# Attention-and-experts block: depthwise convolution moved to TensorE, windows paired, v placed by ScalarE

## What is computed

```
qkv = einsum('oi,bihw->bohw', qkv_w, xh); q, k, v = split(qkv, 3)
lepe = conv_general_dilated(v, lepe_w, (1, 1), 'SAME', feature_group_count=c)
attn = softmax(einsum('nhqc,nhkc->nhqk', q * scale, k) + bias)
out = einsum('nhqk,nhkc->nhqc', attn, v) + lepe        # windows of 16 tokens, 8 heads
x = x + out(plain) + unroll(out(rolled))
t = t + sum over the 2 best experts of gate * (norm(t) @ expert_w + expert_b)
```

## Time and profile before

| | |
|---|---|
| median of 3 runs | 3483.31 us (3472.05 to 3487.70) |
| profiled execution, span | 3495.3 us; its own time stands nowhere else |
| busy: PE, DVE, ACT, POOL | 3038.4, 3088.6, 2038.3, 2932.3 us |
| busy share of PEld | 54% |
| mean granted TensorE clock | 0.925 |
| DMA | 469.79 MB, 427432 packets |

### The profile page before, as it was taken

The page is one execution under the profiler, slowest core; times in us unless marked ns, Lnnn a source line. Parts: engine busy times, 40 slices in busy tenths (PEclk is TensorE's granted clock), DMA queues, the critical chain, the costliest instruction groups (busy, mean ns, idle before and its releaser), DMA issues.

```text
span 3495.3 us, 200950 instructions
## 1 busy us (share of the span) xinstructions
PE 3038.4 (87%) x82372; PEld 1892.0 (54%) x82372; DVE 3088.6 (88%) x6049; ACT 2038.3 (58%) x4130; POOL 2932.3 (84%) x5382
## 2 busy tenths in 40 slices
PE   5889888888898888998888988889899899889886
PEld 3655555555555555555555555555555555555551
DVE  3789999889999888998999889999899899999995
ACT  3666666556565556665666656566556656666651
POOL 5998888888898788987888878889788988888970
PEclk8999999999899899998999989999899989999986
DMA  2345555545555455545555544555455555555555
GB/s 58 85 122 147 137 143 138 143 130 143 136 144 139 125 144 137 145 130 133 136 139 140 139 131 130 143 135 143 130 140 138 143 134 145 137 143 137 138 124 151
DMA packets 427432, 469.79 MB, mean 134 GB/s; under 512 B 117616, under 2 KB 407920, under 8 KB 426480
## 3 DMA queue, kind: packets, MB, share of 16 engines
q1 hardware_dynamic: 260592, 342.97, 36.3%
q0 software_dynamic: 165888, 113.57, 13.5%
HBM read 264.97 MB, written 77.86 MB: 98 GB/s over the span
## 4 chain that ended last, share of the span: by engine, by line
PE 36%; DVE 22%; issue 14%; DMA 12%; SPq 9%; POOL 3%; ACT 3%; DVEq 1%; ACTq 0%; POOLq 0%
PE bank L585 9%; PE bank L652 8%; SPq L454 6%; DMA gate_wide<-gate_rows 6%; DVE lepe L896 6%; DMA z<-fin 5%; PE bank L570 5%; DVE row_max L904 3%; PE bank L658 2%; PE bank L612 2%; POOL vx L528 2%; PE bank L624 2%; DVE probT L969 2%; SPq L449 1%; DVE gx L884 1%
## 5 line engine op out<-in xcount | busy, mean ns | idle before, releaser
L528 POOL DMA_DIRECT2D vx<-vt x3072 | 1555.5, 515 | 201.9 <-PE bank L658 181.0
L652 PEld LDWEIGHTS bank<-probT,vx 128*32 128x32 f32 x36864 | 825.8, 188 | 442.4 <-issue 378.2
L652 PE MATMUL bank<-probT,vx 128*32 128x16 f32 x36864 | 888.2, 234 | 170.7 <-issue 117.5
L516 POOL DMA_DIRECT2D kx<-k_sb x1536 | 738.8, 488 | 230.9 <-issue 114.6
L585 PEld LDWEIGHTS bank<-kx,qx 32*32 32x32 f32 x36864 | 602.9, 112 | 434.9 <-issue 432.2
L585 PE MATMUL bank<-kx,qx 32*32 32x64 f32 x36864 | 709.9, 227 | 128.5 <-issue 90.9
L742 ACT ACTIVATE prob<-prob 128x512 f32<-128x512 f32 x576 | 367.4, 638 | 538.9 <-DVE prob L909 538.6
L896 DVE SCALAR_TENSOR_TENSOR lepe<-vpad,table,lepe 128x384 f32<-128x384 f32 x960 | 630.8, 657 | 0.0
L884 DVE TENSOR_TENSOR gx<-gate_wide,yn_pair 128x768 f32<-128x768 f32 x384 | 393.8, 1026 | 194.4 <-DMA gate_wide<-gate_rows 148.0
L547 POOL TENSOR_TENSOR lepe_p<-lepe_p,tap_sb 128x384 f32<-128x384 f32 x384 | 435.0, 1133 | 39.0 <-issue 18.5
L904 DVE TENSOR_REDUCE row_max<-bank 128x32 f32<-128x512 f32 x576 | 394.4, 685 | 29.5 <-PE bank L585 16.4
(11 more groups left out here) (75 smaller groups left out, 3801.9 us busy)
## 6 DMA issues: line engine op xcount, KB each, us to landing
gate_wide<-gate_rows SPq DMA_DIRECT2D x768, 192.0 KB
vx<-vt POOLq DMA_DIRECT2D x3072, 12.0 KB
kx<-k_sb POOLq DMA_DIRECT2D x1536, 24.0 KB
z<-fin SPq DMA_DIRECT2D x192, 192.0 KB, 4.3
yn_pair<-yn POOLq DMA_DIRECT2D x384, 96.0 KB
xa<-in_x SPq DMA_DIRECT2D x192, 96.0 KB, 3.3
xn<-xa SPq DMA_DIRECT2D x192, 96.0 KB
xs<-xn SPq DMA_DIRECT2D x96, 192.0 KB
```

Of the source, the lines that this page charges most:

```text
L516: pool.dma_start(kx[to + m:to + C:4, r % 2, m, :], k_sb[at + m:at + C:4, r % 2, :])\
L528: pool.dma_start(vx[to:to + TOK, r % 2, col:col + 13:4, odd, :], vt[at:at + TOK, r % 2, x::2, :, :].rearrange("p h n k -> p h (n k)"))\
L652: last = MM(bank_o[32 * c:32 * c + 32, at * TOK:(at + 1) * TOK], vx[:, kr % 2, :, at % 2, at // 2 * 4 + ba], probT[:, kr % 2, at, ba * TOK ...
```

## The change

The convolution becomes 12 matmuls a tile on TensorE (`conv`, 4 in each of three slots: one for each column offset, two groups of taps, two halves of the image's width). They work on the normalised x: `conv_w` holds v's weights times the taps, made once at the start, and `halo` holds 10 rows of x, twice, one row apart, so that one matmul takes two rows of taps. The plain and the rolled convolution are added in the weights. The first and last tile of an image take other weights at some rows and are cut in pieces (`conv_rows`). The result is added to y from its own bank (`bank_c`), and VectorE makes three additions of a tile (y_first, y_second, y_third) in place of two. All that carried the taps leaves: `wo`, `vpad`, the tap products, GpSimd's additions, the multiply-adds and `add_taps`.

The 8 windows of a unit are now 4 of the left half of the image and the 4 that lie half a width to the right. A block of the turned probabilities then holds two windows (squares), and the weights of a product matmul are 32 floats in a row. The zeros of `vx` are no longer left by DMAs of parts: ScalarE copies all of v into its place by 8 copies a strip with a mask (1 or 0 per partition) as the scale, 3, 3 and 2 of them in three slots, between the exponential and the placing of the bias. Product and scores are written in pieces of 4 x 4 and 4 x 16 floats. The row sums take 8 matmuls of half the columns.

Bank g goes to the convolution, so turned logits and turned gates use p1, the gates in one transpose of 48 columns, and `logits` moves from slot 42 to 44. x, the output and z have a layout in halves, so that a tile loads by 5 DMAs (7 in the first tile) and stores by 1; the halo takes 2 loads (4 at an image's edges).

```diff
 LAG = dict(
...
-    tap_products=15, pool_taps=16, taps=19, add_taps=24,
-    store_z=24, load_tile=33, y_first=37, y_second=38, tile_sum=39, tile_variance=40, router=41, logits=42,
-    take_logits=43, gates=45, gap_exp=46, turn_gates=47, pair_yn=47, store_gates=48, spread_gates=49,
+    store_z=24, load_halo=29, load_tile=33, conv=34, y_first=37, y_second=38, y_third=38, tile_sum=39, tile_variance=40, router=41, logits=44,
+    take_logits=44, gates=45, gap_exp=46, turn_gates=47, pair_yn=47, store_gates=48, spread_gates=49,
...
-        vx = sb("vx", [128, 2, 32, 2, WIN // 2 * 4])
+        vx = sb("vx", [128, 2, PAIRED, HEADS, 32])
...
-                if st := s.strip("spread_v"):
-                    k, r = st
-                    wait_alone(pool, vt_made, k + 1)
...
-                                pool.dma_start(vx[to:to + TOK, r % 2, col:col + 13:4, odd, :],
-                                               vt[at:at + TOK, r % 2, x::2, :, :].rearrange("p h n k -> p h (n k)"))\
-                                    .then_inc(v_spread[r % 2], 16)
...
                     MM(bank_p[0][:, 0:SPX], wv, xs[:, r % 4, :], start=True, stop=True).then_inc(v_made, 1)
-                    if r % 2:
-                        pe.wait_ge(ln_made, tiles_to(s, (k - 1) // 2 + 3))
-                    MM(bank_p[1][:, 0:SPX], wo, xs[:, r % 4, :], start=True, stop=True).then_inc(vo_made, 1)
...
+                if (ti := s.in_tile("conv")) and ti[2] < len(SIDES):
+                    k, r, side = ti
...
+                    for group, skip in ((0, 0), (1, 2)):
+                        for top, end, which in conv_rows(t)[group]:
+                            for y_ in range(2):
+                                low, high = y_ * HALFW + max(0, -dw - y_), (y_ + 1) * HALFW - max(0, dw + y_ - 1)
+                                last = MM(by_rows(bank_c[y_ * C:(y_ + 1) * C, 0:SPX], HALFW)
+                                          [:, top:end, low - y_ * HALFW:high - y_ * HALFW],
+                                          conv_w[:, which, group * 3 + side, :],
+                                          by_rows(halo[:, r % 2, :], W)[:, top + skip:end + skip, low + dw:high + dw],
+                                          start=first[y_], stop=(side == 2 and group == 1), skip_group_check=True)
...
-                    for w in range(UW):
-                        at = (j * UW + w)
-                        for c in range(4):
-                            ba = c % 2 * 2 + c // 2
-                            last = MM(bank_o[32 * c:32 * c + 32, at * TOK:(at + 1) * TOK],
-                                      vx[:, kr % 2, :, at % 2, at // 2 * 4 + ba],
-                                      probT[:, kr % 2, at, ba * TOK:(ba + 1) * TOK], start=True, stop=True)
+                    for n in range(j * UPAIR, (j + 1) * UPAIR):
+                        for a in range(2):
+                            cols = slice(a * (SPX // 2), (a + 1) * (SPX // 2))
+                            for m in range(4):
+                                last = MM(out_window(bank_o[32 * m:32 * m + 32, cols], n), vx[:, kr % 2, n, m * 2 + a, :],
+                                          probT[:, kr % 2, n, m, a * TOK:(a + 1) * TOK]
+                                          .rearrange("p (i x) -> p i x", x=SP), start=True, stop=True)
...
                     S.activation(prob[:, r % 4, :], prob[:, r % 4, :], ACT.Exp).then_inc(exp_made, 1)
+                if st := s.in_strip("spread_v"):
...
+                    for part in range(3 * j, min(3 * j + 3, V_PARTS)):
+                        g, y_ = part // 2, part % 2
+                        at, col = slice(g * CH, g * CH + CH), y_ * TOK + g * HD
+                        S.activation(vx[at, r % 2, :, :, col:col + HD].rearrange("p n k h -> p (n k) h"),
+                                     vt[at, r % 2, :, :, :].rearrange("p n k h -> p (n k) h"), ACT.Copy,
+                                     scale=const("mask_v")[at, y_:y_ + 1]).then_inc(v_spread, 1)
                 if u := s.unit("place_bias"):
...
-                if st := s.in_strip("tap_products"):
...
-                if taps:
-                    tap(taps[0], taps[1], 2 * taps[2] + 1)
```

More of the change, by code:

```diff
@@ L48 @@
 UNITS = WIN // UW
+PAIRED = WIN // 2
+UPAIR = UW // 2
+HALFW = W // 2
 UPX = UW * TOK
@@ L206, in lay_tables @@
         rows = slice(g * CH, (g + 1) * CH)
-        for h in range(HD):
-            for m in range(HEADS):
-                a, b, y = m // 4, m // 2 % 2, m % 2
+        for place in range(HEADS):
+            a, m = place // 4, place % 4
+            head = (place - roll * ROLL) % HEADS
+            for h in range(HD):
                 for part, name in ((0, "wq"), (1, "wk")):
-                    put(name, rows, g * CH + a * 16 + h * 4 + m % 4, qkv_w[part * CH + h * HEADS + m])
-                here = (h - 1) % HD if roll and a and b else h
-                one = qkv_w[2 * CH + here * HEADS + m]
-                put("wv", rows, g * CH + h * 8 + y * 4 + b * 2 + a, one)
-                at = (a * 2 + b) * CH + roll * 16 + h * 4 + half * 2 + y
-                put("wo", rows, at, one)
-                put("taps", at, slice(0, 9), lepe_w[here * HEADS + m].reshape(9))
@@ L226, in lay_tables @@
     order = tile_channels()
+    for col, channel in enumerate(order):
+        half, o = channel // CH, channel % CH
+        for roll, name in ((0, "plain"), (ROLL, "rolled")):
+            own = (o - roll) % CH
+            for i in range(CH):
+                for copy in range(2):
+                    put("v_" + name, copy * C + (half * CH + i + roll) % C, col, qkv_w[2 * CH + own, i])
+            taps = lepe_w[own].reshape(3, 3)
+            for side in range(3):
+                dw = SIDES[side] + 1
+                put("taps_" + name, slice(0, C), side * C + col, taps[0, dw])
+                put("taps_" + name, slice(C, 128), side * C + col, taps[1, dw])
+                put("taps_" + name, slice(0, C), (3 + side) * C + col, taps[2, dw])
```

345 lines of the change are left out of this document (187 added, 158 removed).

## The result

The changed kernel takes 3820.45 us (median of 4 runs) where the kernel before took 3485.51 in the same session: ratio 1.0948, 95% interval 1.091 to 1.0985. The changed kernel is slower, as forecast, but by 9.5% and not by the 2.1 to 2.5% forecast; 3811 lies outside the range of 3430 to 3750 us. The profiled execution has a span of 3800.9 us.

What follows compares the result with a forecast made beforehand. It took VectorE, TensorE and GpSimd as close together, none alone at its limit; afterwards TensorE's work 2976 + ends 75.5 + loop turns 48 + ScalarE waits 385 + small waits 85 = 3570 us, range 3430 to 3750.

Steps and rivals of the forecast that it cites:

- TensorE's own work: TensorE's 3038.4 us, less v product 157.4, gate transposes 34 and faster product 346, plus convolution 475: 2976 us.
- pipeline's ends: TensorE idle in the pipeline's first 80 and last 105 us: 75.5 us, kept from the profile before.
- TensorE waits for ScalarE (bias, k copy): Scores waiting for the placed bias and the tile-sum matmul for bank p1: 4.0 us a tile, 385 us.
- loop turns: TensorE idle where the loop turns to the next image: about 6.9 us each, seven turns, 48 us.
- small waits: A quarter of TensorE's other 333 us of waits stays as semaphore waits, 85 us; the rest ends with VectorE's load.
- The mechanism, its two places: ScalarE's copies between exponential and bias stall TensorE at score matmuls and the tile-sum matmul, some 3 to 5 us a tile.
- the experts' pair as the model: Two experts' matmuls of the convolution's shape take 0.80 us, so six pairs a tile take 4.8 us.
- Rival 3: Product and score matmuls that write in pieces are slower: 3935 us, chance 0.07.
- Rival 2: Weights in a row give nothing, as their loads lie behind other work: 3743 us, chance 0.11.
- the six slots: ScalarE's path against TensorE's work per slot of a tile: waits 2.0 (value), 1.2 (tile sum), 0.8 us (variance), others nothing.
- second value slot: The value slot with two convolution pairs: TensorE's 4.2 us of work against ScalarE's 4.0, so no wait.
- rival 1: Weights in a row gain more and copies cost less, so the kernel gets faster: 3400 to 3460 us, chance 0.24.

Runs made afterwards that it cites:

- copies_last: The changed kernel with the eight copies into vx moved from before the placing of the bias to the end of ScalarE's slot: 3539.81 us, ratio 1.0171.
- whole_rows: The changed kernel with product and score matmuls writing whole rows instead of pieces, results in wrong places: 3811.73 us, ratio 1.0917.
- strided: The changed kernel, copies unchanged, with TensorE reading a product's weights 96 floats apart from the same buffer, so wrong values: 3870.55 us, ratio 1.1101.
- copies_full: The changed kernel with each of the eight copies over all 128 partitions, using an eight-column mask: 3736.96 us, ratio 1.0751.
- before_in_row: The kernel before, with only TensorE's reading of a product's weights changed to 32 columns in a row, so wrong values: 3493.26 us, ratio 1.0029.
- best: last_k with the copies over all 128 partitions and the bias placed just ahead of the exponential: 3458.34 us, ratio 0.9884.
- last_k: copies_last with ScalarE's k copy put ahead of the two q copies of its slot: 3494.95 us, ratio 1.0016.
- few_conv: The changed kernel with 10 of the 12 convolution matmuls of a tile left out: 3707.09 us, ratio 1.0625.
- apart_rows: The changed kernel with vx's 32 columns stored outside, weights 96 floats apart, and copies reading in pieces and writing whole rows: 4206.36 us, ratio 1.2052.

## Why the prediction was right in direction and wrong in size

The forecast was 3570 us. Its sum against the profiled span of 3800.9 us, term by term:

| term | forecast | measured |
|---|---|---|
| TensorE's own work | 2976 | 3013.6 |
| pipeline's ends | 75.5 | 77.1 |
| TensorE waits for ScalarE (bias, k copy) | 385 | 504.9 |
| loop turns | 48 | 31 |
| small waits | 85 | 174 |

The ends come from two windows of the changed kernel (0 to 80 and 3690 to 3801 us), 191.00 - 113.88, which answer to the earlier trace rows; 8 us of the waits for ScalarE lie in these windows too. The small waits are what is left of the span.

```profile
sum 191.00, PE 113.88 PEld 53.55 DVE 79.99 ACT 52.69 POOL 29.80; mean PE 56.94 PEld 26.78 DVE 39.99 ACT 26.34 POOL 14.90
```

**Right.** The mechanism, its two places, and the side: copies_last shows it by moving nothing else. As forecast came VectorE under 2458 us (2233.6), GpSimd under 1377 (937.2), the copies near 0.6 us long (0.604), the convolution's 475 us (482.5), the experts' pair as the model for it. Rival 3 is refuted by whole_rows. The Trainium skill, "PSUM — Partial Sum Buffer", section "Specifications (TRN2)", would have these pieces slow the matmuls significantly. The trace does not agree: 742 against 739 us for the scores. Rival 2 falls with the product's 468 us. By the rule of the Trainium skill, "TensorE: Matmul & The Clock Gate", section "LDWEIGHTS (loading the stationary operand)", that a load's time goes by its columns, loads of 32 columns would last equally long. The traces do not agree: they take 157 ns in strided and 115 ns with the columns in a row.

**Wrong: the waits for ScalarE.** The step that failed most is the one on the six slots, with the copy's spacing of 0.51: 385 us forecast, 504.9 measured. In the tile shown above, value slot 2.31 us (forecast 2.0), tile sum 1.28 (1.2), variance 1.47 (0.8), second value slot 0.66 (nothing). Both sides of each comparison were off.

- ScalarE's path was longer. Value matmul to score takes 1852.85 - 1848.52 = 4.33 us and 1871.04 - 1866.67 = 4.37, not 4.0; variance matmul to score 1864.85 - 1860.34 = 4.51, not 4.2. The exponential and three copies take 2.29 us to the bias's start (1852.10 - 1849.81), not 2.07. The forecast took the copy's price from tap products that all begin at the same partition; copies_full, with the partitions alone changed, shows 69 to 74 us for that.
- TensorE had less to do meanwhile. The second value slot's 4.2 us were 3.67 (1848.52 to 1851.38 + 0.81), the variance slot's 3.4 were 3.04 (1860.34 to 1862.54 + 0.84). The main reason is the product: 468.2 / 576 = 0.81 us a unit instead of 0.94, and 0.60 from its first matmul to the next instruction (1851.38 - 1850.78) where I counted 0.90. "Nothing" in the second value slot hung on 0.2 us, and that was gone.

So a third of the extra gain that rival 1 hoped for did come (420 us off the product, against 346), and most of it went into waits, as strided shows: 231 us of product, 53 to 59 us of time. Rival 1 priced the extra gain at about half; a quarter would have been right.

**Wrong: loop turns and small waits.** The loop's body runs six times, so it turns five times and not seven; the turns cost 31 us. For the small waits I kept a quarter of 333 us with no reason for the quarter. Before the change 228 us of TensorE's idle time were of the kind that the profile calls issue, the turns among them, and 201 us are after it: they did not end with VectorE's load.

**Wrong, smaller: TensorE's own work.** With the measured product and convolution the sum would be 3038.4 - 157.4 - 34 + 482.5 - 420 = 2910, yet TensorE is busy 3013.6 us. Some matmuls that did not change have grown: the scores from 709.9 to 741.7 us, the tile-sum matmul from 110.7 to 125.7, and q and k, which run side by side, from 208 to 240 (the union of their records; here q, before and after):

```profile
L624 PE MATMUL bank<-xs,table 32*32 32x384 f32 x1536 | 200.1, 545 | 5.2 <-issue 3.8 <-ACT vpad L737 1.3
```

```profile
L664 PE MATMUL bank<-xs,table 32*32 32x384 f32 x1536 | 227.4, 635 | 7.8 <-issue 6.4 <-ACT v_sb L800 1.3
```

Together these are busy some 76 us longer. The v product saved less than its 157.4 us, too: it began some 0.16 us before the value matmul ahead of it had ended (0.91 us long in the earlier trace rows, 0.75 to the next start), which is 31 us in 192 strips. The mean granted clock is 0.902, before it was 0.925, but the growth is not spread as the mean would have it: the experts' matmuls have become shorter (542 to 533 ns). What grew is the matmuls that wait for ScalarE and those right behind them, and the tile above shows them at half the clock behind its longest wait. I had no term for that. How much of the 76 us the clock explains is not shown.

**Wrong: what bounded the kernel before.** "No engine alone at its limit" was right, but I made the sum on TensorE's work plus waits, as if each microsecond taken from it counted unless it was counted again as a wait. before_in_row shows that 320 us off TensorE were worth nothing there. The sum fits the changed kernel as far as it does only because the change took VectorE's load and the DMAs off the path as well: VectorE has 9% of the chain that ended last, DMA and SP 2%.

Left open: why the product of before, with weights 96 floats apart, took 888 us and that of strided, also 96 apart, 699; and what the profile calls issue, 99.6 us before scores here and 187.4 in best.

## What to carry to other kernels

Work that moves to an engine with room is priced by what stands behind it in that engine's order, not by its busy share: eight copies ahead of the instruction that TensorE waits for cost some 270 us more than at the end of the slot, where they cost no more than on another engine. When two engines alternate in such a loop, time each slot on both sides, and expect most of a gain on the side that waits already to go into the wait. Before you price a saving at full value, look at which engines share the chain that ended last: a 320 us saving on one at 87% was worth nothing while the chain ran through others.

## What the runs showed of the hardware that I had not expected

- ScalarE: copies of 384 floats last 0.60 us over 32 or 128 partitions. The next instruction starts some 0.1 us before the end; where it begins at another partition it did not in these runs: 0.51 us from one copy to the next against 0.62. Writing single floats 384 bytes apart takes 0.957 us, reading every fourth float and writing rows 0.988.
- Loads of 128 x 32 weights: 115 ns with the columns in a row, 157 with 96 floats between them; the product 468 against 699 us.
- TensorE's granted clock falls to half behind long waits, as in the tile above, and the matmuls that follow get longer. Over whole runs a lower mean clock went with longer score matmuls. From the view of the cores, for last_k, the changed kernel, few_conv and apart_rows in this order:

```profile
core 0: 3475.0 us, clock 0.934
```

```profile
core 0: 3800.9 us, clock 0.902
```

```profile
core 0: 3705.7 us, clock 0.865
```

```profile
core 0: 4198.3 us, clock 0.852
```

The scores' mean is 223, 234, 241 and 246 ns there. The idle share alone does not set the mean clock: TensorE is idle for 21% of both the changed kernel and apart_rows. A wait can thus cost a second time, and a wait removed gives something back: TensorE's busy time is 2946.8 us in best and 3013.6 in the changed kernel, for the same matmuls.
